# Pass 1 of a macaron layer's experts, planned in four parts of one group each instead of three parts, the first of two groups

## The reference

```python
B, S, D = 32, 256, 128          # 8192 tokens
def ffn(x):                     # E = 8 experts, K = 2, H = 512
    scores = softmax(x @ Wg + bg)
    topk_probs, topk_idx = top_k(scores, 2)
    h = gelu(einsum('nd,edh->enh', x, W1) + b1[:, None, :])
    eo = einsum('enh,ehd->end', h, W2) + b2[:, None, :]
    return einsum('nk,nkd->nd', topk_probs, take(eo, topk_idx))
def attn(x):                    # q, k, v = x @ Wq, x @ Wk, x @ Wv in 16 heads
    k_win, v_win = windows of 9 positions ending at each query
    wts = softmax(masked(einsum('bhsd,bhswd->bhsw', q, k_win) / 0.56))
    return einsum('bhsw,bhswd->bhsd', wts, v_win) @ Wo
x = x + 0.5 * ffn(layernorm(x))      # pass 0
x = x + attn(layernorm(x))
x = x + 0.5 * ffn(layernorm(x))      # pass 1
```

## Time and profile before

| what | us |
|---|---|
| median of 3 runs | 1211.37 |
| lowest, highest | 1206.4, 1219.11 |
| profiled execution, its own time | 1195.72 |
| span in its profile | 1193.9 |
| busy PE, PEld, DVE | 919.0, 762.5, 644.4 |
| busy ACT, POOL | 500.2, 669.9 |

### The profile page before, as it was taken

The page is one execution under the profiler, slowest core; times in us unless marked ns, Lnnn a source line. Parts: engine busy times, 40 slices in busy tenths (PEclk is TensorE's granted clock), DMA queues, the critical chain, the costliest instruction groups (busy, mean ns, idle before and its releaser), DMA issues.

```text
span 1193.9 us, 22506 instructions
## 1 busy us (share of the span) xinstructions
PE 919.0 (77%) x6345; PEld 762.5 (64%) x6345; DVE 644.4 (54%) x1309; ACT 500.2 (42%) x1215; POOL 669.9 (56%) x593
## 2 busy tenths in 40 slices
PE   3446868567897798988898838998988868865984
PEld 3334747456775587777777725677766756754874
DVE  6655133423147587898979998687851511110222
ACT  4433524334534273655644415634434433322432
POOL 2475445446387766455668556356765555555452
PEclk9999769889898799999999978989985988897997
DMA  8813212252113421026112121223222223432683
GB/s 274 235 55 73 55 44 50 65 137 67 42 58 62 134 54 41 19 59 139 33 39 55 23 96 55 45 52 68 50 60 53 51 59 84 116 97 69 154 190 120
DMA packets 170344, 96.44 MB, mean 81 GB/s; under 512 B 137696, under 2 KB 154390, under 8 KB 169332
## 3 DMA queue, kind: packets, MB, share of 16 engines
q1 hardware_dynamic: 152276, 59.29, 21.9%
q0 software_dynamic: 17952, 35.71, 9.5%
HBM read 25.77 MB, written 52.35 MB: 65 GB/s over the span
## 4 chain that ended last, share of the span: by engine, by line
PE 41%; issue 16%; DMA 10%; POOL 9%; another core or an unknown queue 8%; DVE 6%; SPq 6%; ACT 3%; ACTq 0%; POOLq 0%; DVEq 0%
PE bank L966 18%; PE bank L949 12%; POOL x_sorted L579 7%; DMA x_sorted<-hl,slots_all 5%; PE bank L854 3%; DMA x_sb<-in_L_attn_x 2%; PE bank L960 2%; ACT h_f L756 1%; POOL y_pairs L596 1%; SPq L476 1%; PE bank L840 1%; PE bank L867 1%; SPq L466 1%; SPq L452 1%
## 5 line engine op out<-in xcount | busy, mean ns | idle before, releaser
L596 POOL DMA_INDIRECT y_pairs<-y_sb,tile_ids x305 | 359.5, 1179 | 330.0 <-issue 215.9
L756 ACT ACTIVATE h_f<-bank,b_cols 128x256 f32<-128x256 f32 (+1 forms) x736 | 264.1, 439 | 443.3 <-PE bank L949 298.3
L579 POOL DMA_INDIRECT x_sorted<-hl,slots_all x256 | 301.9, 1179 | 179.4 <-issue 86.8
L966 PE MATMUL bank<-w_sb,h_f 128*128 x2440 | 355.2, 299 | 22.6 <-issue 15.3
L966 PEld LDWEIGHTS bank<-w_sb,h_f 128*128 128x128 f32 x2440 | 315.3, 206 | 45.1 <-issue 28.2
L949 PE MATMUL bank<-xsT,w_hl 128*128 128x256 f16 (+1 forms) x2208 | 263.3, 270 | 56.6 <-issue 20.9
L949 PEld LDWEIGHTS bank<-xsT,w_hl 128*128 x2208 | 201.2, 104 | 93.8 <-issue 66.7
L1412 DVE TENSOR_TENSOR y_sb<-bank,tile_ids 128x256 f32<-128x256 f32 (+1 forms) x184 | 68.8, 375 | 342.2 <-PE bank L966 169.0
L960 PE MATMUL bank<-b_hl,ones_b 64*128 x184 | 49.5, 269 | 72.8 <-DVE y_sb L1412 59.8
L960 PEld LDWEIGHTS bank<-b_hl,ones_b 64*128 64x128 f16 x184 | 17.1, 93 | 113.2 <-issue 110.6
L1197 DVE TENSOR_TENSOR prod<-score,qkv 128x2304 f32<-128x2304 f32 x32 | 81.6, 2550 | 0.2
(11 more groups left out here) (159 smaller groups left out, 851.3 us busy)
## 6 DMA issues: line engine op xcount, KB each, us to landing
y_in<-y_pairs SPq DMA_DIRECT2D x28, 512.0 KB
x_sorted<-no_rows SPq DMA_DIRECT2D x7, 720.0 KB
y_pairs<-y_sb,tile_ids POOLq DMA_INDIRECT x305
x_sb<-in_L_attn_x SPq DMA_DIRECT2D x4, 1024.0 KB, 5.7
x_sorted<-hl,slots_all POOLq DMA_INDIRECT x256
x_sorted<-no_rows SPq DMA_DIRECT2D x56, 72.0 KB
out<-x_sb SPq DMA_DIRECT2D x3, 1024.0 KB
xsT<-x_sorted SPq DMA_TRANSPOSE x184
```

The costliest lines, as they stand in the source:

```text
L579: pool.indirect_dma_start(out=x_sorted[p], out_offset=bass.IndirectOffsetOnAxis(ap=slots_all[:, at:at + 1], axis=0), in_=hl[:, c % 2, i // ...
L596: pool.indirect_dma_start(out=y_pairs, out_offset=bass.IndirectOffsetOnAxis(ap=tile_ids[:, t.n % IDS, i, 0:1].bitcast(U32), axis=0), in_=y ...
L756: ins = act.activation(h_part(t, b)[:, k, :], bank[h_banks.uses[u][0]][:, k * t.slots:(k + 1) * t.slots], ACT.Gelu, bias=b1_cols[:, bass.d ...
L966: ins = pe.matmul(into[:, half, :], h_part(t, c // t.per)[:, c % t.per, half * P:(half + 1) * P], w2_flat[:, bass.ds((e * HC + c) * D, D)] ...
```

## The change

`SPLITS` gives pass 1 four parts of one group. Parts 4 to 7 then have 24 tiles each (t96 to t119, t120 to t143, t144 to t167, t168 to t191), so there are 192 tiles and 312 blocks where there were 184 and 305; one wide tile fewer and nine narrow ones more. One more plan is made (and none for 40 tiles), one more table has its spare rows cleared at the start, and 8 more tails are cleared. No function is changed. All five order strings are replaced.

```diff
-SPLITS = (((0,), (1,), (2,), (3,)), ((0, 1), (2,), (3,)))
+SPLITS = (((0,), (1,), (2,), (3,)), ((0,), (1,), (2,), (3,)))
...
 POOL_ORDER = (
-    "sssssyysyysyyyyyyyyyyyyyysyyyyyysyyyyyyyyyysyyyyyyyyysysysyyyyysyyyyyyyyyysyyysyyyyyyyyyyyyyssssssssyyyyyyyyyy"
...
+    "ssssssyyyyyyyyyyyyysyyyyysyyyyysyyyyyyyyysyyyyyyyyyyysyyyyssysyyyyyyysyyyyysyyyyyyyyyyyyyyyyyyyyyysyyysyysysys"
...
```

54 lines of the change are left out of this document (28 added, 26 removed).

## The result

The changed kernel took 1214.32 us (median of 20 runs, 1206.46 to 1231.79), the kernel before 1208.70 us in as many (1196.89 to 1220.56): a ratio of 1.0055, 95% interval 1.0031 to 1.0080. The ratio is worked out from fast runs alone and is not the quotient of the two medians, 1.0046. The kernel is slower by half a per cent, where 1.75% faster was forecast. The profiled execution took 1215.08 us with a span of 1213.3 us. The one of before, from which the prediction was worked out, was shorter than each of its 20 timed runs (1195.72). So the two traces differ by 19 us where the medians differ by 6, and a few us of what follows belong to the executions and not to the change.

A forecast was written before the change was run, and what follows sets the result against it. TensorE was taken as nearest the bound, VectorE close behind. Attention's end at 926 + 152 to t168 + 95 for the last part = 1173 us of span against 1193.9 (−1.75%), so 1190 us; range 1167 to 1219.

The forecast's parts named there:

- t144's start: From attention's end to t144: 46 us, as before, with about 20 us of idle TensorE.
- five bursts: Group 3's last row bursts, in a row behind t162, 7.0 us each; TensorE waits 33 us before t168.
- the last part: From t168's first matmul to the end: 79 us for 24 tiles and 16 to store, 95 in all.
- Ahead of attention: Before group 0's first product: moved tiles, scatters and one more cleared area cost nothing, between −10 and +3 us.
- Term 1: Attention ends later: 884 + 58 for 31 more blocks − 23 idle filled + 7 for GpSimd = 926 us.
- 23 are filled: In group 2's attention window, 33 us of idle TensorE: blocks fill 23, some 10 stay.
- Term 3: From t144 to t168: first matmul of t168 152 us after attention's end, after a wait of 33 us.
- the rival: Group 2's window: filled idle time raises the clock from 0.89 to 0.99; span 1150, time 1167 us; chance 0.19.
- No gain to be told: Groups 1 and 2 under attention: engines don't fill each other's gaps, 308 us for 294; time 1204 us; chance 0.25.
- The slower case: Under attention GpSimd becomes the bound: attention ends at 958, span 1205, time 1223 us; chance 0.13.
- The rule that a scatter waits out a product: GpSimd under attention: scatters starting with a 2.55 us VectorE product wait all of it; 31 blocks cost up to 79 us.
- point of no change: An attention end of 947 us would mean no change in time; 959 would mean slower by 1%.

The follow-up runs named there:

- The emptied scatters: One result scatter instead of two per wide tile: t96 to t134 of the changed kernel, 0.9944; t96 to t114 of the kernel before, 0.9937.
- The parts alone: Kernel before with the change's eight parts, every engine's steps kept at their old places: 1.0335 (1251.5 us) on the slow chip, 1.0297 on the quick.

## Why the prediction was wrong, step by step

The forecast's span was 1173 us and the trace's is 1213.3. Of these 40 us, 8 lie ahead of attention, 2 in its windows, 26 between attention's end and t168, and 4 in the last part.

**Right.** The plan of which tile stands where, to within one tile; TensorE's work (14 us more for seven blocks on the slow chip, 13 forecast, though only 4 on the quick one); t144's start 46 us after attention's end (38 on the quick chip); five bursts of 33 us ahead of t168; the last part, 99 us from t168's first matmul to the end (95 forecast, 90 on the quick chip).

**Ahead of attention** was costed at nothing, between −10 and +3 (two of the 31 blocks stand there, but were counted in term 1), and is +8 (331 to 339), and +5 on the quick chip: outside its bound. I had said pass 0 ends otherwise by over 10 us if I am wrong; it is 8. What makes it was not taken apart; TensorE's work grew by 1.6 us there and its idle time by 6.

**Term 1** came out nearly right by luck, by two errors. 31 × 1.88 − 23 + 7 = 42 us; the four windows grew by 44. But TensorE's work in them grew by 49 us and not 58 (29 of the 31 blocks stand in them, 55 us at that price), and its idle time fell by 5 and not by 16. The step that failed is "23 are filled". The gap itself was filled, but group 2's window keeps 22 idle us where 10 were to stay, and the other windows, which were to keep theirs but for the 7 us of GpSimd, gained 6. The prediction cost the wait at group 0's last burst at nothing; TensorE is idle for 8 of the 19 us from 672 to 691, as shown above, on both kinds of chip. The emptied scatters show GpSimd as another part of what holds the windows (7 us each), the plan on VectorE a third: the text named every move in the order and left out that a part more is a plan more on VectorE, some 30 small instructions and 7 to 10 us, in the very window whose VectorE is 112 of 127 us busy.

**Term 3** is where the sum broke: 106 us forecast from t144 to t168, 133 measured. I let t144 to t162 run at 1.88 us a block without a pause, the rate of the last part: 34 blocks, 64 us to t162's result. It took 91 us. 74 of them are TensorE's work, because the granted clock was 0.83 there and 0.96 in the last part (64 × 0.96/0.83 = 74), and 17 are idle, most of it the waits for `y_sb` above. So all that hangs on t162's result comes 28 us late. The earlier trace rows had the warning: from 979 to 1099 TensorE works 82 of 120 us at a clock of 0.85, and only 9.4 of the 38 idle us are the wait ahead of t160. The saving was counted as the whole difference of a stretch at its old idle rate and a new one without it. On the quick chip the error is smaller: t162's result comes after 73 us, with the 64 us of work that were forecast, at a clock of 0.96, and 9 idle. And yet the change loses more there, for the old stretch has less idle time to save as well: 61 us behind attention, not 77.

**The comparison itself.** Behind attention TensorE's idle time was to fall by 18 us. It rose by 4 on the slow chip and by 6 on the quick one (61 to 67). (By a few us traces of one kernel differ in this: it is 81 and 87 in the two unedited traces of the changed kernel on slow chips.) The wait for the last group's rows is not removed by having fewer tiles ahead of it: fewer tiles leave more of the same chain uncovered. That is what the prediction said of t168 ("eats a good part"), with the part taken too small.

**Rivals.** The clock rose where the rival had it rise, in group 2's window, but halfway, from 0.89 to 0.94 and not to 0.99, and over the whole span it fell (0.898 to 0.881). "No gain to be told" had the mechanism, two engines which hand work to each other keep their idle time, and the right size for groups 1 and 2: 309 us measured, 308 there, against 294 in the sum (301 with GpSimd's 7). Its time, 1204 us, is still 10 too short, as it shares the other terms. The slower case's GpSimd bound is not it: attention ended 22 us sooner than there. The rule that a scatter waits out a product would cost GpSimd up to 79 us; by the mean scatter (1.47 us in group 1's window, 0.99 in the last part) 31 blocks cost it 15, because only some scatters meet a product (see the last section). It ended under that case's own point of no change too (936, and 947), and the kernel is slower all the same, because that point rested on term 3.

**What stays open.** The parts alone cost 40 us on the slow chip; about six of them are blocks, about seven the plan. Most of the rest lies in group 3's window, where five blocks more and narrow tiles stand between attention's steps; that window's extra idle time (16 us, 8 on the quick chip) may belong to this arrangement and not to the parts. What the change costs ahead of attention, and how the 22 idle us of group 2's window divide, was not tried. No version that leaves nothing out was faster than the kernel before.

## What to carry to other kernels

Before a gap without tiles is counted as room, make the ledger of the engine that is to fill it, window by window: the window with 92 us without a result held 33 us of idle TensorE, and the tiles and the earlier bursts of rows put there brought idle time of their own. When a transfer moves in an engine's order, look for what else on that order needs its buffer. A split that lets work start earlier also multiplies what is done once per part (here 7 padded blocks, most likely 6 us, and a plan of 30 small steps on VectorE, 7 us of attention), and each of these was as large as the half per cent in question; price it first. And price moved work at the rate and the clock of the stretch that it lands in, never at those of the cleanest stretch.

## What the hardware showed

**Two speeds of the same program.** The kernel before took 1079 to 1080 us on two chips and 1197 to 1211 us on two others and when the change was timed. The GpSimd scatters are alike (results' scatters 1165 ns in the mean on the quick chip, 1179 ns in the slow chip's trace). The granted clock is 0.926 and 0.898 over the profiled spans, and 0.97 and 0.88 ahead of attention; but the eight parts alone reached attention at 259.5 us on the quick chip at 0.87, so this clock doesn't set the time. What stands out is TensorE with nothing to wait for. The waits of TensorE from 100 to 250 us, on the slow chip:

```profile
PE bank L949 <- issue: 13.9, 15, 1.9
PE bank L966 <- issue: 12.0, 13, 2.0
```

and on the quick one, where the only "issue" row is

```profile
PE bank L960 <- issue: 0.2, 1, 0.2
```

On the slow chip, while GpSimd issues scatters one behind the other, TensorE issues one to four matmuls and pauses, mostly about every 1.4 to 1.5 us; the scatters' own step is 1.29 us:

```profile
157.16 0.98 POOL L596 DMA_INDIRECT y_pairs<-y_sb,tile_ids  x1 [0.30 <-issue]
...
158.44 0.98 POOL L596 DMA_INDIRECT y_pairs<-y_sb,tile_ids  x1 [0.30 <-issue]
159.16 0.37 PE L949 MATMUL bank<-xsT,w_hl 128*128 128x256 f16 x1 [1.36 <-issue]
...
159.73 0.98 POOL L596 DMA_INDIRECT y_pairs<-y_sb,tile_ids  x1 [0.30 <-issue]
...
160.67 0.37 PE L949 MATMUL bank<-xsT,w_hl 128*128 128x256 f16 x1 [1.14 <-issue]
```

In the same 16 us of the quick chip's trace the scatters stand as densely, and TensorE runs 12 and 16 matmuls without a pause. What holds it on the slow chip was not tried, nor whether it stays with the chip. Ahead of attention the two kinds differ by 69 us (331 and 262), of which 20 are TensorE's work and 49 its idle time; the waits shown are 26 of the 49. This may have changed the size of the result (1.0036 to 1.0055, and 1.0115, with intervals that overlap), but not its sign.

**The clock and short waits.** The same tiles of part 6 with bursts between them ran at a granted clock of 0.79 instead of 0.96, and their matmuls took 82.5 us instead of 72.7. Idle time scattered through a stretch cost 10 us of work beside itself. The slow chip shows the same without an edit: 34 blocks of t144 to t162 took 74 us of work at 0.83 with 17 idle us among them, and 64 us on the quick chip at 0.96 with 9.

**A scatter waits out a product on VectorE.** Half of the result scatters take about 0.98 us, and some take up to 3.3 us. In the trace of the kernel before, 56 scatters (of rows and of results) start while one of the 2.55 us products runs, and every one of them ends 0.8 to 0.9 us after that product's end; in the changed kernel's it is 56 of 59. One such pair, the product ending at 519.28 and the scatter at 520.14:

```profile
516.73 2.55 DVE L1152 TENSOR_TENSOR prod<-qkv 128x2304 f32<-128x2304 f32 x1
517.66 2.48 POOL L597 DMA_INDIRECT y_pairs<-y_sb,tile_ids  x1 [14.01 <-DVE y_sb L1413]
```

So the 0.5 us that a scatter costs under attention is a mean of many at nothing and some at up to 2.4 us.
